# Gated attention in fp32: the products with the maxima as four 32-row tiles behind the scores of a round, and the order of ScalarE's copies

## What is computed

```python
xn = _layernorm(x)                                   # x: (4, 1024, 128)
Q, K, V = ((xn @ W).reshape(n, s, 16, 64) for W in (Wq, Wk, Wv))
attn = softmax(einsum('bshe,bthe->bsth', Q, K / 8), axis=2)
A = gelu(einsum('bsth,bthe->bshe', attn, V).reshape(n, s, 1024), approximate=False)
s = xn + A @ Wpost
g = silu(quantised(xn) @ quantised(weight).T + bias) # fp6 grid, blocks of 32 with a scale
out = x + s * g
```

## Time and profile before

| | |
|---|---|
| median of 3 runs | 1596.32 us (1595.92 to 1597.55) |
| profiled execution, its time | 1595.06 us |
| profiled execution, its span | 1593.3 us |
| mean granted TensorE clock | 0.979 of full |
| TensorE products busy | 1472.8 us |
| GpSimd busy | 1146.8 us |
| VectorE busy | 1127.2 us |
| ScalarE busy | 754.6 us |

### The profile page before, as it was taken

One profiled execution on the slowest core, in us unless ns is written; L12 is line 12 of the kernel. 1 busy time (PEld: TensorE's weight loads), 2 busy tenths in 40 slices (PEclk: granted clock), 3 DMA queues, 4 the chain that ended last, 5 costly groups with the idle time before them and its releaser, 6 DMA issues. The chain is left out here.

```text
span 1593.3 us, 24618 instructions
## 1 busy us (share of the span) xinstructions
PE 1472.8 (92%) x9857; PEld 798.5 (50%) x9857; DVE 1127.2 (71%) x1469; ACT 754.6 (47%) x925; POOL 1146.8 (72%) x528
## 2 busy tenths in 40 slices
PE   3998899999999899999999899999999999999578
PEld 1554455555454455554555445555555555555277
DVE  5577877777777777777777777777777777777312
ACT  1444445544454445544445444454444544444253
POOL 0587687788877777787787678877888777888500
PEclk8899999999999999999999999999999999999789
DMA  2000010000000010000000000000000000000297
GB/s 84 1 9 8 16 42 9 16 16 16 16 8 16 16 35 16 16 16 14 9 16 16 9 29 16 16 8 16 16 16 16 9 16 16 16 16 16 69 346 254
DMA packets 43136, 52.11 MB, mean 33 GB/s; under 512 B 2832, under 2 KB 24720, under 8 KB 43024
## 3 DMA queue, kind: packets, MB, share of 16 engines
q1 hardware_dynamic: 42384, 48.44, 9.0%
q0 software_dynamic: 640, 2.10, 0.4%
HBM read 27.46 MB, written 23.07 MB: 32 GB/s over the span
## 5 line engine op out<-in xcount | busy, mean ns | idle before, releaser
L510 POOL TENSOR_TENSOR prob_sum<-prob_sum,probs 128x1024 f32<-128x1024 f32 x384 | 912.8, 2377 | 283.1 <-ACT probs L435 255.0
L621 DVE TENSOR_REDUCE half_maxes<-peaks 128x2 f32<-128x1024 f32 x512 | 621.1, 1213 | 279.4 <-PE peaks L314 278.1
L435 ACT ACTIVATE probs<-scores 128x1024 f32<-128x1024 f32 x512 | 498.0, 1023 | 469.7 <-PE scores L332 469.6
L341 PE MATMUL acc<-probs,vals 128*64 128x512 f32 x2048 | 490.3, 600 | 0.0
L314 PE MATMUL peaks<-k_hi,q_hi 64*128 64x512 f32 x1024 | 233.1, 449 | 49.3 <-DVE half_maxes L621 48.1
L341 PEld LDWEIGHTS acc<-probs,vals 128*64 128x64 f32 x2048 | 138.0, 137 | 249.7 <-issue 215.4
L637 DVE RECIPROCAL inv_sum<-inv_sum 128x128 f32<-128x128 f32 x256 | 240.0, 941 | 10.0 <-ACT inv_sum L419 10.0
L510 POOL TENSOR_TENSOR prob_sum<-probs 128x1024 f32<-128x1024 f32 x64 | 151.4, 2365 | 73.3 <-ACT probs L435 70.7
L328 PE MATMUL scores<-q_hi,k_hi 64*128 64x512 f32 x1024 | 202.9, 392 | 0.0
L328 PE MATMUL scores<-q_lo,k_hi 64*128 64x512 f32 x1024 | 202.6, 391 | 0.0
L332 PE MATMUL scores<-max_rows,ones_r 64*128 64x512 f32 x1024 | 202.5, 390 | 0.0
(11 more groups left out here) (98 smaller groups left out, 947.5 us busy)
## 6 DMA issues: line engine op xcount, KB each, us to landing
att_scratch<-att SPq DMA_DIRECT2D x64, 256.0 KB, 2.0
att_in<-att_scratch SPq DMA_DIRECT2D x32, 512.0 KB, 8.2
x_in<-in_L_attn_X SPq DMA_DIRECT2D x4, 512.0 KB, 5.1
xn_scratch<-xn SPq DMA_DIRECT2D x4, 512.0 KB, 3.6
gate_scratch<-gate SPq DMA_DIRECT2D x32, 64.0 KB, 1.5
x_res<-in_L_attn_X SPq DMA_DIRECT2D x8, 256.0 KB, 5.0
xn_res<-xn_scratch SPq DMA_DIRECT2D x8, 256.0 KB, 6.2
out_dram<-res POOLq DMA_DIRECT2D x8, 256.0 KB, 5.7
```

The costliest lines, as they stand in the source:

```text
L341: last = mm(acc[own[h], :], vals[(s // 2) % 2][:, j, own[h]], probs[j][:, h, :], start=(j == 0), stop=(j == KT - 1), tile_position=col[h])
L435: sa.activation(probs[j][:, :, :], scores[j % 2][:, :, :], ACT.Exp, scale=DH ** -0.5).then_inc(probs_ready, 1)
L510: gp.tensor_tensor(prob_sum[s % 2][:, :, :], before[:, :, :], probs[j][:, :, :], ALU.add).then_inc(probs_summed, 1)
L621: v.tensor_reduce(half_maxes[:, :, f // 2, f % 2], peaks[:, :, :], AX.X, ALU.max).then_inc(peaks_read, 1)
```

## The change

Three things. First, the pair with the maxima leaves `score`; a new `lower(s, r)` does it for both groups of keys at once, behind the round's second `peak` and ahead of the extra work. It is four products with 32 rows each, on four row tiles of the array: two heads times two groups. For that, the maxima have to stand in each head's 64 rows twice, so `join_maxima` writes them to columns 0 to 3 and 32 to 35, and `neg_identity` repeats every 32 rows. Second, both groups' `scores_ready` are now given behind `lower`. Third, ScalarE's first copy of a round stands between the two exps of that round.

```diff
@@ def score(s, j)
-                if j == 0:
+            def lower(s, r):
+                if r == 0:
                     is_read(pe, ("turn", s))
-                for h in (0, 1):
-                    last = mm(w[:, h, :], ones_r[own[h], :], max_rows[s % 2][own[h], :], start=False, stop=True, tile_position=row[h])
-                last.then_inc(scores_ready, 1)
+                for j in (0, 1):
+                    for h in (0, 1):
+                        at = h * DH + j * (DH // 2)
+                        rows = slice(at, at + DH // 2)
+                        last = mm(scores[j][:, h, :], ones_r[rows, :], max_rows[s % 2][rows, :], start=False, stop=True,
+                                  tile_position=(at, 0))
+                    last.then_inc(scores_ready, 1)
@@ TensorE, a round
                     if s + 1 < NS:
                         peak(s + 1, 2 * r + 1)
+                    lower(s, r)
                     for use in before:
                         run(use)
@@ ScalarE, a round
                     exps(s, 2 * r)
+                    if half == 0:
+                        if r < 2 and ahead:
+                            high(("qk"[r], n + 1, 0))
+                        if r == 2 and s > 0:
+                            copy_sums(s - 1)
+                    else:
+                        if r == 0 and ahead:
+                            copy_v(("v", n + 1, 0))
+                        if r == 1 and n == 0:
+                            copy_square(("w",), ffn_wT)
+                        if r == 1 and n > 0:
+                            copy_sums(s - 1)
                     exps(s, 2 * r + 1)
@@ VectorE, join_maxima
-                v.tensor_reduce(maxes[:, :, 0:QT], half_maxes[:, :, :, :], AX.X, ALU.max).then_inc(maxima_ready, 1)
+                twice = maxes[:, :, :].rearrange("p h (c k) -> p h c k", c=2)[:, :, :, 0:QT]
+                v.tensor_reduce(twice, half_maxes[:, :, :, :].unsqueeze(2).broadcast_to([P, 2, 2, QT, 2]), AX.X, ALU.max
+                                ).then_inc(maxima_ready, 1)
@@ inputs
-    add("neg_identity", -np.tile(np.eye(64, 4, dtype=np.float32), (2, 1)))
+    add("neg_identity", -np.tile(np.eye(32, 4, dtype=np.float32), (4, 1)))
```

More of the change, by code:

```diff
@@ L452, in _ @@
                     exps(s, 2 * r)
-                    exps(s, 2 * r + 1)
[L454 to L463, removed]
-                            copy_v(("v", n + 1, 1))
@@ new lines, in _ @@
+                    exps(s, 2 * r + 1)
+                    if r == 0 and s > 0:
+                        copy_acc(s - 1)
+                    if half == 0:
+                        if r < 2 and ahead:
+                            high(("qk"[r], n + 1, 1))
+                        if r == 2 and n > 0:
+                            copy_square(("turn_x", n - 1), quant_T)
+                        if n % HP == 2 and later < B:
+                            if r == 1:
+                                square(later)
+                            if r == 2:
+                                root(later)
+                    else:
+                        if r == 0 and ahead:
+                            copy_v(("v", n + 1, 1))
+                        if r == 1 and n == 0:
@@ L472, in _ @@
                             copy_sums(s - 1)
-                        if half == 1 and n % HP in (4, 5) and later < B:
+                        if r == 1 and n % HP in (4, 5) and later < B:
                             copy_xT_later(("x", later, n % HP - 4))
[L475 to L483, removed]
```

## The result

The changed kernel takes 1676.88 us in the median of 4 runs (1674.05 to 1679.95), the kernel before 1596.85 (4 runs): a ratio of 1.050, 95% interval 1.048 to 1.053. It is 5% slower. The forecast was 1649 with a range of 1602 to 1680: the direction was right and the time lies in the range, 28 us above the point. What those 28 us are, the windows show first.

What follows compares the result with a forecast made beforehand. TensorE's own sequence was taken as the bound, with VectorE bounding in a few places. From the profiled 1595.06 us, 50.6 + 2 + 0.5 gave 1648.2; with 1.26 for the median, 1649 us, range 1602 to 1680.

Steps and rivals of the forecast that it cites:

- (2): In a round, VectorE's reduction holds the second `peaks` pair to 1.82 us after the start instead of 1.72, load uncovered.
- c: Microseconds of tiling changes around the four products' slot in a round; 0.31 taken, bounds 0 and 0.65.
- (3): The four 32-row products take one slot of 0.23 us; the next stage starts at 2.39 + c instead of 2.49.
- (a): Rival: changing from 64-row to 32-row tiles costs nothing, only the way out, c = 0.10; 1609 us; chance 16%.
- (b): Rival: the 32-row products cost nothing around them, c below 0.044; 1590 us with c = 0; chance 10%.
- (c): Rival: the four products are dearer; loads in two turns 1671 us (12%), products in two turns 1693, both 1714 (8%).
- (5): Sum over rounds: 127 x 0.21 + 63 x 0.38 = 50.6 us; stalls in odd steps' rounds 2 and 3 absorb 0.21.
- (7): `join_maxima` on VectorE writes 16 columns for 8, 32 times on the path: +0.5 us.
- (6): In the three head pairs with a layer norm, about a dozen rounds with held `peaks` grow more: +2 us.
- (8): ScalarE's later exps and the copy between them still leave TensorE 1.0 us to spare: nothing added.
- (d): Rival: TensorE waits for ScalarE's late second exp, +50 us, 1700 us; 6% together with everything else.
- (9): GpSimd gets probabilities 1.3 to 2.2 us later; 8.6 us idle in two steps cover it: nothing added.

Runs made afterwards that it cites:

- The short reductions: Both kernels with the first quantising operation reading PSUM and VectorE's `peaks` reduction over half the columns: 1545.47 us (kernel before), 1543.63 us (changed).
- the run with the new cut: Kernel before, all work kept, with an odd step's ten quantising operations cut as two ahead of round 2's second reduction, four behind it, four in round 3: 1585.06 us.

## Why the prediction was right, and where it was too low

- **Held `peaks` pair (2), right.** 1.83 instead of the 1.82 worked out, load uncovered, as in the earlier trace rows. In round 0 the pair starts 2.00 after the round's start (821.22 against 819.22), forecast 1.99, and that round grew by 0.36, forecast 0.38. The short reductions show that this hold decides.
- **c = 0.31 (3), right within 0.02.** 2.39 + c came out as 2.68. There is a change from 64-row to 32-row tiles that costs, so rival (a) falls; (b) falls with it, and the four products are one slot (0.43 to the next stage), so (c) falls too. The Trainium skill, "TensorEngine Tiling (Array Packing)", Key Properties, had it so (a change of mode drains), and the trace agrees for 64 to 32 rows: 0.42 from a held pair to the four products, 0.34 without a change.
- **The sum of (5) to (7), right in kind and 13% too high.** 50.6 + 2 + 0.5 = 53.1 forecast; 46.8 between the two kernels when the quantising operation is out of it. The ordinary rounds grew by 0.17 to 0.20 and not 0.21, rounds 0 by 0.35 and 0.36 and not 0.38.
- **The layer norm's rounds (6), mis-sized.** In the profiled execution the three head pairs with one grew from 166.4 to 177.3 us, 3.4 more than three ordinary ones, where 2 was forecast. The account of it was too simple: the held pairs moved both ways (round 2 from 6.20 to 4.31, round 1 from 3.44 to 4.00 after the start), and the granted clock of these pairs fell from 0.97 to 0.91, 0.91 and 0.86. The prediction had no term for the clock.
- **ScalarE (8), right.** TensorE's wait for `probs` didn't become a stall; (d) falls. The load of the scores' weights waits 2.4 us for `probs` in all, and as much with the old order. So it isn't the moved copies that keep this wait away; what they save is the wait of the second projections for the low parts.
- **GpSimd (9), wrong.** "I put both at nothing", with the 8.6 us of idle time of GpSimd as cover. The delay that I had named, 1.3 to 2.2 us, was right (the addition shown starts 3.88 after round 1's start instead of 2.57), and GpSimd did catch it up (the sums' products wait 5.0 us for it in all, 4.0 before). But its additions also block a VectorE operation while they run, and in the one round where VectorE is the bound the later end of an addition is a later end of that operation: 0.60 to 1.56 us in the mean, 32 x 0.96 = 31 us. This term was missing from the sum. The runs with one SBUF input size it in medians: 41.3 for it in the changed kernel less 7.7 in the one before, 33.6, beside the 46.8 without it. So the 28 us above the point are 34 that were missing, less 6 by which the rest was too high. That 53 + 31 = 84 comes so near to the 84.9 by which the span grew is partly luck: 53 was 6 too high, and the profiled execution of the changed kernel is the slowest of its four (the medians are 80.0 apart). With the edit, round 2 of odd steps takes 4.60 in both kernels, where it took 5.00 and 6.14. The rows had it: the 0.69 us of an operation whose neighbours of the same size take 0.29 to 0.30 was in view, and I took it as its length.
- **That 1677 lies in the range is in part luck.** The upper end of 1680 stood for dearer loads, the first case of (c), which did not come. Nothing in the range was meant for GpSimd's additions.
- **The cover of rounds 2 and 3 of odd steps (5), half right.** The 0.21 did go into the stall; the length of 5.00 that I called VectorE's was not constant, since it had GpSimd's addition in it.

## What to carry to other kernels

A product that looks redundant in a stream may be the cover for something that a single buffer makes serial: before it is moved out, add up what lies between the two uses of that buffer (here 1.72 against 1.82 needed). Fewer slots by narrower tiles are worth their place only if the slots saved cost more than the changes of tiling around them (here 0.56 us for two pairs against 0.51 for the four tiles with their change, and nothing of it in the time). And when an engine's work is shifted in time, ask not only who waits for its results but which operations of another engine can't run while it runs; an operation that takes longer than its equals of the same size points to one.

## What the runs showed of the hardware that I had not expected

- A VectorE product of two SBUF tiles of 128x128 took 0.29 us alone and up to 1.94 us beside GpSimd's additions, ending 0.16 us after one. The chain's other operations of that size, with at most one input in SBUF, took 0.29 to 0.30, and so did this one beside an addition once it had one input in SBUF.
- In the run with the new cut TensorE's granted clock fell after stalls of 2.48 and 3.85 us in otherwise dense work: to half, 1.2 of 2.4 GHz, for the products of the next microseconds (0.79 us for a `peaks` pair that takes 0.50, weighing 3.68 instead of 1.94), so that the run with the new cut has a mean of 0.969 where the kernel before has 0.979. In the kernel before, the clock fell to half after its stalls of 3.86 us too (a weighing of 2.63), and stayed full after those of 2.24 to 2.27. In the changed kernel, stalls of 2.11 and 2.12 us were followed by half clock once in three times, and those of 2.41 to 2.43 each time; so the length of a stall alone doesn't tell what the clock does. A stall that the clock follows costs more than its own length.
